# A state-space stage's slots: the scaling of the transposed tile goes from GpSimd to VectorE, the low part of the gated output from VectorE to GpSimd

## What is computed

```python
def step(h, ins):                       # one token, 48 heads of 64 features, state 128 x 64
    x_t, B_t, C_t, dt_t = ins
    dA = jnp.exp(A * dt_t)[..., None, None]
    h = dA * h + B_t[..., :, None] * x_t[..., None, :]
    y_t = jnp.einsum('bhnp,bhn->bhp', h, C_t) + D_param[None, :, None] * x_t
    return (h, y_t)
...
y = _rms(y, inner_norm_w)
y = y * jax.nn.silu(z)
out = y @ out_proj_w.T
```

## Time and profile before

| | us |
|---|---|
| three runs | 3154.69, 3155.89, 3159.99 |
| median | 3155.89 |
| profiled execution, from first to last instruction (span) | 3143.6 |
| median of the runs less that span | 12.3 |

### The profile page before, as it was taken

How to read it: one execution, slowest core, us unless ns; L and a number is a source line. 1 busy time by engine, 2 the same in 40 slices (tenths; PEclk the granted TensorE clock), 3 DMA queues, 4 the chain that set the end, 5 groups by cost and what they waited for, 6 DMA issues and landing times. The chain is left out here.

```text
span 3143.6 us, 57164 instructions
## 1 busy us (share of the span) xinstructions
PE 2684.3 (85%) x17166; PEld 2104.5 (67%) x17166; DVE 2377.4 (76%) x5287; ACT 2126.3 (68%) x4766; POOL 1944.0 (62%) x1644
## 2 busy tenths in 40 slices
PE   3699889987399387397479999999999999999998
PEld 2366666665299245287268788787787878878786
DVE  2466666766456289555379999999899999999997
ACT  3454455433355266365279999999899999999996
POOL 2322222216200254423369999999999999999998
PEclk8799999898799688698689999999999999999998
DMA  5455545447633753556476666665866667666563
GB/s 134 121 168 167 169 168 186 165 155 245 190 120 125 249 162 122 180 180 204 138 239 213 203 219 202 208 220 188 245 202 206 213 204 220 202 221 207 189 216 121
DMA packets 318736, 588.34 MB, mean 187 GB/s; under 512 B 46934, under 2 KB 140534, under 8 KB 317942
## 3 DMA queue, kind: packets, MB, share of 16 engines
q1 hardware_dynamic: 306150, 551.12, 55.1%
q0 software_dynamic: 12288, 33.57, 3.3%
HBM read 464.66 MB, written 124.05 MB: 187 GB/s over the span
## 5 line engine op out<-in xcount | busy, mean ns | idle before, releaser
L2593 POOL TENSOR_TENSOR mm<-mt,cb 128x512 f32<-128x512 f32 x384 | 492.8, 1307 | 42.4 <-ACT mt L2542 39.0
L2523 ACT ACTIVATE mt<-a_wide,a_tok 128x128 f32<-128x128 f32 x1536 | 486.5, 389 | 0.5
L2679 DVE SCALAR_TENSOR_TENSOR cv<-bank,taps,cv 128x509 f32<-128x509 f32 (+2 forms) x576 | 429.5, 746 | 13.6
L59 PE MATMUL bank<-f,wi 128*128 128x512 f32 x768 | 321.2, 418 | 16.3 <-DMA wi<-ssm_wi_split 16.3
L2614 POOL TENSOR_TENSOR yz<-y,zs 128x512 f32<-128x512 f32 x192 | 310.7, 1618 | 15.1
L60 PE MATMUL bank<-f,wi 128*128 128x512 f32 x768 | 305.0, 397 | 0.0
L61 PE MATMUL bank<-f,wi 128*128 128x512 f32 x768 | 304.9, 397 | 0.0
L2610 POOL TENSOR_TENSOR y<-t 128x512 f32<-128x512 f32 x192 | 245.8, 1280 | 1.6 <-DVE t L2726 1.6
L2438 PE MATMUL bank<-xd,b_tok 128*128 128x128 f32 x1536 | 223.5, 289 | 21.5 <-POOL xd L2600 20.3
L2624 POOL TENSOR_TENSOR y<-y,ys 128x512 f32<-128x512 f32 x184 | 237.7, 1292 | 3.2 <-ACT ys L2536 3.2
L1772 POOL DMA_INDIRECT fr_ring<-expert_scratch,disp_place x64 | 67.9, 1061 | 276.0 <-POOLq L79 244.2
(11 more groups left out here) (455 smaller groups left out, 7941.7 us busy)
## 6 DMA issues: line engine op xcount, KB each, us to landing
wi<-ssm_wi_split SPq DMA_DIRECT2D x192, 512.0 KB
a_wide<-a_scratch SPq DMA_DIRECT2D x192, 512.0 KB, 5.7
l_fw<-ffn_split SPq DMA_DIRECT2D x72, 768.0 KB, 4.6
ea<-ea_scratch SPq DMA_DIRECT2D x384, 128.0 KB, 3.2
wo<-ssm_wo_split SPq DMA_DIRECT2D x192, 256.0 KB, 3.7
ssm_wi_split<-l_s_out SPq DMA_DIRECT2D x24, 512.0 KB
sorted_scratch<-fr_zeros SPq DMA_DIRECT2D x4, 3072.0 KB, 25.2
ey_x<-sorted_scratch SPq DMA_DIRECT2D x96, 128.0 KB
```

The source lines that it names most:

```text
L59: pe.matmul(out, wh, xh, start=first, stop=False)
L2523: i = act.activation(mt[:, h, chunk(j)], a_wide[:, g % R, h, chunk(j)], ACT.Relu, bias=a_tok[:, s * NJ + j, 2 * t + h:2 * t + h + 1], scal ...
L2593: pl.tensor_tensor(mm[:, :, ts], mt[:, :, ts], cb[:, js, :].rearrange("p j t -> p (j t)") .unsqueeze(1).broadcast_to([P, 2, TS // 2]), ALU ...
L2679: dve.scalar_tensor_tensor(cv[:, a:TS], bank[:, X, 0:TS - a], taps[:, t, k:k + 1], cv[:, a:TS], ALU.mult, ALU.add).then_inc(ph["tap"], 1)
```

## The change

`to_end`, which makes xd, leaves GpSimd's loop for VectorE's. There it reads the transposed tile from bank XT in place of x_tok, and stands first in the next beat's list, ahead of `convolve`. It still waits for x_tok (ScalarE has then read the bank) and for the update of the slot before. `output_low`, which makes y_lo, leaves VectorE's loop for GpSimd's, where it stands in the place of `to_end`, behind `decayed` and ahead of `outputs`. Since bank XT now has one more reader, the three that write it next (ScalarE's tanh, TensorE's transposes and mean of squares) wait for xd; ScalarE's `tokens` no longer does.

```diff
--- before.py
+++ after.py
@@ -2462,12 +2462,14 @@
                 def mean_square(s):
                     done(pe, "y2", s * NCT + LAST)
                     done(pe, "x_tok", min(s * NCT + LAST + 3, N - 1))
+                    done(pe, "xd", min(s * NCT + LAST + 3, N - 1))
                     done(pe, "xs", min(s * NCT + LAST + 4, N - 1))
                     pe.matmul(bank[:, XT, :], col("mean_di"), y2[:], start=True, stop=True).then_inc(ph["yms"], 1)
 
                 def turn(g):
                     done(pe, "xs", g)
                     done(pe, "x_tok", g - 1)
+                    done(pe, "xd", g - 1)
                     s, t = g // NCT, g % NCT
                     if t >= 3:
                         done(pe, "yr_ln", s - 1)
@@ -2528,6 +2530,7 @@
                 def tanh(g):
                     done(act, "tap", g, NR)
                     done(act, "x_tok", g - 1)
+                    done(act, "xd", g - 1)
                     act.activation(bank[:, XT, :], cv[:], ACT.Tanh).then_inc(ph["th"], 1)
 
                 def square(g):
@@ -2549,7 +2552,6 @@
                 def tokens(g):
                     done(act, "xt", g)
                     done(act, "intra", g - 1)
-                    done(act, "xd", g - 1)
                     act.activation(x_tok[:].rearrange("p j c -> p (j c)"), bank[:, XT, :], ACT.Copy).then_inc(ph["x_tok"], 1)
 
                 def inverse_norm(s):
@@ -2593,14 +2595,10 @@
                         pl.tensor_tensor(mm[:, :, ts], mt[:, :, ts], cb[:, js, :].rearrange("p j t -> p (j t)")
                                          .unsqueeze(1).broadcast_to([P, 2, TS // 2]), ALU.mult).then_inc(ph["mm"], 1)
 
-                def to_end(g):
-                    s, t = g // NCT, g % NCT
-                    done(pl, "x_tok", g)
-                    done(pl, "u", g - 1)
-                    pl.tensor_tensor(xd[:].rearrange("p j (h c) -> p j h c", h=2),
-                                     x_tok[:].rearrange("p j (h c) -> p j h c", h=2),
-                                     w_tok[:, s * NJ:(s + 1) * NJ, 2 * t:2 * t + 2].unsqueeze(3)
-                                     .broadcast_to([P, NJ, 2, PH]), ALU.mult).then_inc(ph["xd"], 1)
+                def output_low(g):
+                    done(pl, "y_hi", g)
+                    done(pl, "out", g - 1)
+                    pl.tensor_tensor(y_lo[:], yz[:, g % 2], y_hi[:].bitcast(F32), ALU.subtract).then_inc(ph["y_lo"], 1)
 
                 def outputs(g):
                     done(pl, "t2", g)
@@ -2654,7 +2652,8 @@
                 for k in BEATS:
                     if has(k - 1):
                         decayed(k - 1)
-                        to_end(k - 1)
+                    if has(k - 4):
+                        output_low(k - 4)
                     if has(k - 3):
                         outputs(k - 3)
                         squares(k - 3)
@@ -2725,10 +2724,14 @@
                     done(dve, "y", g - 1)
                     dve.tensor_tensor(t1[:], bank[:, INTER, :], ea[:, g % R], ALU.mult).then_inc(ph["t1"], 1)
 
-                def output_low(g):
-                    done(dve, "y_hi", g)
-                    done(dve, "out", g - 1)
-                    dve.tensor_tensor(y_lo[:], yz[:, g % 2], y_hi[:].bitcast(F32), ALU.subtract).then_inc(ph["y_lo"], 1)
+                def to_end(g):
+                    s, t = g // NCT, g % NCT
+                    done(dve, "x_tok", g)
+                    done(dve, "u", g - 1)
+                    dve.tensor_tensor(xd[:].rearrange("p j (h c) -> p j h c", h=2),
+                                      bank[:, XT, :].rearrange("p (j h c) -> p j h c", j=NJ, h=2),
+                                      w_tok[:, s * NJ:(s + 1) * NJ, 2 * t:2 * t + 2].unsqueeze(3)
+                                      .broadcast_to([P, NJ, 2, PH]), ALU.mult).then_inc(ph["xd"], 1)
 
                 def evacuate(s):
                     done(dve, "out", s * NCT + LAST)
@@ -2744,11 +2747,10 @@
                     e = k - 5
                     if has(e) and e % NCT == LAST:
                         evacuate(e // NCT)
+                    if has(k - 1):
+                        to_end(k - 1)
                     if has(k):
                         convolve(k)
-                    if has(k - 4):
-                        output_low(k - 4)
-                    if has(k):
                         gate(k)
                         silu(k)
                     if has(k - 1):
```

## The result

| | runs | median | least to greatest |
|---|---|---|---|
| before | 20 | 3154.42 | 3139.38 to 3181.13 |
| after | 20 | 3139.88 | 3129.17 to 3148.25 |

The ratio after to before is 0.9948, with an interval of 0.9933 to 0.9962: faster by 0.5%, some 16 us by this ratio (the two medians lie 14.5 apart). The profiled execution of after took 3139.94 us, its span is 3138.2.

A forecast was written before the change was run, and what follows sets the result against it. GpSimd was taken to set the pace at 7.72 us a slot: 182 slots by -0.11 is -20, +1 for slice changes, +1 for the last slots, total -18; span 3125.6 plus 12.3 gives 3138, range 3122 to 3156.

The forecast's parts named there:

- GpSimd's terms: GpSimd's slot: y_lo replaces xd for +0.23, yz falls by 0.35, net -0.11 us, giving a slot of 7.61.
- estimate of 1.335: y_lo on GpSimd: 1.335 us by the skill's ratio of 1.96 on 0.681, making the sum -0.07 a slot.
- Rival 3: GpSimd's yz keeps its 1.63 us because y_lo does not stretch it; +42 us, 3198; chance 0.04.
- margin of 0.04: From y's end to the next mm: 2.54 us on ScalarE against 2.58 on GpSimd, so ScalarE is just not late.
- rival 1: Another loop takes over and nothing is won; slot stays at 7.70 to 7.74, 3152 to 3160 us; chance 0.14.
- TensorE 7.48: TensorE's slot falls from 7.69 to 7.48 us because its 0.21 wait for xd goes.
- VectorE 7.47: VectorE's slot with xd in and y_lo out, including a new wait of some 0.16 us for the tanh.
- sum of 7.31: VectorE's slot before the new tanh wait: 7.48 less 0.77 for y_lo plus 0.60 for xd.
- Rival 2: xd on VectorE costs 1.05 us as on GpSimd; VectorE's slot 7.83, +20 us, 3176; chance 0.06.
- estimate of 1.03: xd on VectorE: 1.03 us by the skill's rule, if repeating a word counts as a hop.
- Changes of slice and the tail: Delayed xd at slice changes: +1 us over seven; y queueing behind y_lo in the last slots: +1, from -1 to +3.
- distance of 12.3: Gap in us between the profiled span 3143.6 and the median 3155.9 of the runs shown, kept for the forecast.

The follow-up runs named there:

- e4: The changed kernel with VectorE's xd reading x_tok in SBUF instead of bank XT; 3317.94 us, 1.0223 of the kernel before.
- e11: The kernel before with y_lo moved to GpSimd and xd left on GpSimd too; 3317.72 us in a single run.
- e12: The changed kernel with y_lo back on VectorE, between convolution and gate; 3191.59 us in a single run.
- e1: The changed kernel run again unchanged; 3221.85 us, 0.9939 of the kernel before on its chip.
- e10: The changed kernel run again unchanged on another chip; 3136.45 us, 0.9961 of the kernel before.
- e6: The changed kernel with TensorE's product of y_lo with the output weights left out; 3150.72 us in a single run.
- e5: The kernel before run again as a variant of its own; 3153.11 us, 1.0005 of the kernel before.
- e2: The changed kernel with y ahead of y_lo in GpSimd's list; 3202.91 us, 0.9882 of the kernel before.
- e7: The changed kernel with y ahead of y_lo on GpSimd and TensorE's product of y_lo left out; 3101.78 us in a single run.

## Why the prediction was right or wrong

**The whole.** 3138 was forecast, 3139.88 measured, in the range and on the right side. The way there was not right in all its steps, and some of the agreement is luck: the slots gave less than half of what was counted for them, and part of the measured gain lies where no profile shows it.

**GpSimd's terms: right.** y_lo 1.29 (1.286), yz down by 0.35 (0.33), net -0.11. GpSimd's own slot is 7.62 by the profile of after (7.68 less the 0.06 of idling); 7.61 was forecast. Where GpSimd holds the slot, in the edge slots, in which mm follows without a pause, the time fell by 0.11. The estimate of 1.335 by the ratio of the Trainium skill (GPSIMD Engine Reference, 3.1 and 4.1) was too high; y2's row was the better source. Rival 3 falls with yz's own duration, e4 and e11; e12 adds that it is beginning beside y_lo that costs yz its 0.33.

**The margin of 0.04 between GpSimd and ScalarE: the step that failed.** It set 2.54 on ScalarE, from y's end to the next mm, against 2.58 on GpSimd. ScalarE took 2.64: 0.53, 1.30, and 0.81 for the exponential and both handovers (0.03 ahead of the square, 0.78 from the exponential's start to mm's), where 0.72 were put down. No row had shown the first exponential by itself. GpSimd's side was as forecast, 2.64 less the 0.06. The same 2.64 stands, in the median of the plain slots, in e1, e10, e6, e4 and e11. So y_lo ahead of y put a ring of 7.68 to 7.71 in GpSimd's place, and the plain slots got 0.04 instead of 0.11. A slice fell by 1.16 (by 1.02 against e5), and the seven slices from first y to first y by 5 to 8.5 us, where 182 slots were to give 20. The first slice even took 187.6 instead of 186.9. That is rival 1 in part: it named this margin as the closest, and would have had nothing won. The prediction also named GpSimd waiting for the exponentials in most slots as a sign of being wrong; that came, at 0.06 us a time. e2 shows the cause by moving y out of the way of y_lo.

**TensorE 7.48: wrong, and not felt in the changed kernel.** The whole wait of 0.21 for xd was taken as free. 0.17 of it stays as a pause of the weight loads between scores and update for which the trace names nobody, and the step from scores to update fell only from 1.07 to 1.02 (e2). Its own slot is 7.64, 0.08 under the measured 7.72 of before and not 0.24. e6 shows that it doesn't bind in the changed kernel, e2 and e7 that it binds once the ring is gone.

**VectorE 7.47: right.** xd took 0.684 (0.69 forecast, 1.05 the upper bound), xs starts 0.75 after zs and not 0.60, which is the forecast wait for the tanh, and e12 confirms the sum of 7.31 without that wait. In e7 VectorE's slot is 7.47. Rival 2 falls with it. The estimate of 1.03 by the rule of the Trainium skill (Vector Engine (DVE) Microarchitecture Reference, 5.2) falls too: a repeated word doesn't count as a hop here. xd's wait for x_tok is 7.4 us in all, where none was forecast.

**Changes of slice and the tail: the first right, the second open.** The first slot at a change went from 11.29 to 11.45 and the next from 7.90 to 8.08, some 0.3 against the forecast 0.2, while the third and fourth got shorter, so that the four together rose by 0.13; the tanh there waits 1.01 for a convolution that stands behind evacuation and xd:

```profile
1814.07 0.60 ACT L2534 ACTIVATE bank<-cv 128x512 f32<-128x512 f32 x1 [1.01 <-DVE cv L2678]
```

At the end y does queue behind y_lo, as said, but from the start of the last pair of mm to VectorE's end it is 27.0 and 23.4 in the two profiles of before and 25.0, 25.0 and 26.5 in those of after: +1 can't be seen in that.

**The distance of 12.3: misread, without effect.** The profiled execution of after took 1.74 more than its span, that of e5 1.8. The span before was thus that of a run of some 3145, nine below its median. The sum was made against the median in the end, so the error cancels. But it tells what stays open: the profiled runs of before lay 9 and 5 us below their medians, those of the changed kernel within 3, and the stage of these profiles differs by 4 to 11 us while the medians differ by 11 to 16. Some 5 us of the gain are therefore not located. The kernel before also spreads more (42, 32, 20 us from least to greatest, against 19, 14, 14), but no profile of one of its long runs was had.

## What to carry to other kernels

When several engines are all above 90%, add up the rings too, not only each engine's own list: from the instruction on one engine through the handover to the other and back to itself, with every handover in it, and give a margin below 0.1 us no weight. Put what others wait for ahead of what nobody is waiting for yet: y ahead of y_lo is worth as much again as the whole exchange. A VectorE instruction with two SBUF inputs beside a busy GpSimd costs both; look for an input that still lies in PSUM, and if there is none, a time at which no instruction of GpSimd begins beside it spares GpSimd, though not VectorE (e12). Keep in mind that taking away a wait of 0.21 may shorten the slot by 0.05 only, as on TensorE here.

## What the runs showed of the hardware that was not expected

- TensorE's weight loads pause for 0.36 us ahead of the scores, where their width goes from 128 to 64, and for 0.17 us ahead of the update, where it goes back. Both are put down to "issue" and stand in nearly every slot (163 and 170 times from 1750 to 3100 us in the changed kernel), also in e2 where nothing else holds TensorE. The 0.36 stood in the kernel before too (162 times), and in place of the 0.17 it had the wait for xd of 0.21. That the width is the reason is not shown.
- How much two engines hold each other up: xd with both inputs in SBUF 0.963 in the median and 1.82 at most instead of 0.684, the pair of mm beside it 2.97 instead of 2.57, yz beside y_lo 1.63 instead of 1.30.
- Which GpSimd instruction pays. In the kernel before, 187 of 192 y_lo lie over the end of y and the start of yz: y, already running, keeps 1.280 in the median, yz, which begins meanwhile, takes 1.628. In e4 xd lies over the pair of mm, and their medians are 1.300 and 1.735. In e12 y_lo starts while yz is running, and yz keeps 1.275. The VectorE instruction is held up in the median in all three (0.952, 0.963, 0.867).
- An operand spread 64 times along the inner dimension costs VectorE nothing: 677 to 694 ns for 512 elements a partition, t1 678 to 687.
- On GpSimd yz, which reads the y just ahead of it, starts 1.36 after it in the median of the changed kernel's plain slots; the instructions that don't read the one just ahead start 1.23 to 1.26 after it.
